# Four conditioned transformer blocks on one core: attention output of jobs 4 to 14 kept feature-major, divided by sums spread from HBM

## The reference

```python
# block 1 (16 heads of 16; l2-normalised q and k), block 2 (layernorm, 16 heads), block 3 (16 heads, no FFN)
scores = einsum('bhqd,bhkd->bhqk', q, k)
probs  = softmax(scores)                       # block 3: / sqrt(256)
o      = einsum('bhqk,bhkd->bhqd', probs, v)   # then back to [batch, tokens, 256]
x      = x + gate * (o @ proj_w + proj_b)      # blocks 1 and 2; block 3: x + ...
x      = x + gate * (gelu(norm(x) @ w1 + b1) @ w2 + b2)   # blocks 0 to 2
```

## Time and profile before

| | us |
|---|---|
| three executions | 1038.36, 1040.29, 1041.56 (median 1040.29) |
| the profiled execution, its own time | 1039.13 |
| its span, first to last instruction | 1037.5 |
| TensorE matmul busy | 1015.6 (98%) |
| ScalarE busy | 797.7 (77%) |
| VectorE busy | 705.3 (68%) |
| GpSimd busy | 492.5 (47%) |
| mean granted clock of TensorE | 0.997 of 2.4 GHz |

### The profile page before, as it was taken

One profiled execution on the slowest core, in us unless ns is written; L12 is line 12 of the kernel. 1 busy time (PEld: TensorE's weight loads), 2 busy tenths in 40 slices (PEclk: granted clock), 3 DMA queues, 4 the chain that ended last, 5 costly groups with the idle time before them and its releaser, 6 DMA issues.

```text
span 1037.5 us, 19799 instructions
## 1 busy us (share of the span) xinstructions
PE 1015.6 (98%) x6761; PEld 670.7 (65%) x6761; DVE 705.3 (68%) x1436; ACT 797.7 (77%) x1335; POOL 492.5 (47%) x446
## 2 busy tenths in 40 slices
PE   7999999999999999999999999999999999999995
PEld 5789898756657656676566566576666566545442
DVE  7765469563571563547857866967857857999984
ACT  3585756698898899887787887888877877787783
POOL 2563864716556256526346455345353355444241
PEclk9999999999999999999999999999999999999998
DMA  7010001405305132223033222222202203332220
GB/s 261 3 50 12 1 21 45 117 5 133 88 11 144 32 71 66 53 59 72 14 80 99 58 76 63 75 60 54 69 3 63 60 4 98 70 85 57 68 58 26
DMA packets 36386, 64.46 MB, mean 62 GB/s; under 512 B 7208, under 2 KB 22312, under 8 KB 36288
## 3 DMA queue, kind: packets, MB, share of 16 engines
q1 hardware_dynamic: 36288, 63.20, 23.5%
HBM read 22.90 MB, written 2.12 MB: 24 GB/s over the span
## 4 chain that ended last, share of the span: by engine, by line
PE 91%; POOL 2%; issue 2%; DVE 2%; DMA 1%; SPq 0%; ACT 0%; DVEq 0%; POOLq 0%
PE rings L565 17%; PE AVB L677 17%; PE rings L567 15%; PE rings L566 15%; PE rings L664 11%; PE rings L639 7%; PE rings L608 2%; PE rings L717 2%; PE rings L589 1%; PE rings L729 1%; PE rings L647 1%; DMA gT_f<-in_wqkv 1%; PE rings L692 1%; PE rings L627 1%; PE rings L601 1%
## 5 line engine op out<-in xcount | busy, mean ns | idle before, releaser
L876 ACT ACTIVATE probs<-rings 128x512 f32<-128x512 f32 x574 | 303.3, 610 | 85.0 <-PE rings L664 57.8
L1199 DVE TENSOR_REDUCE m<-rings 128x1 fp32r<-128x512 f32 x378 | 239.3, 682 | 52.8 <-PE rings L639 48.0
L677 PE MATMUL AVB<-probs,V 128*32 128x512 f32 x1536 | 200.9, 602 | 0.9 <-issue 0.9
L664 PE MATMUL rings<-SQ,SK 64*128 64x512 f32 x768 | 179.1, 438 | 1.9 <-DMA SQ<-cT 1.6
L1320 POOL TENSOR_TENSOR gT_l<-gT_f,gT_h 128x512 fp32r<-128x512 f32 x96 | 122.0, 1299 | 105.4 <-ACT gT_h L936 104.7
L664 PEld LDWEIGHTS rings<-SQ,SK 64*128 64x128 f32 x768 | 83.5, 184 | 94.5 <-issue 40.5
L639 PE MATMUL rings<-SK,SQ 63*128 63x512 f32 x512 | 129.5, 432 | 0.6 <-DVE m L1196 0.5
L565 PE MATMUL rings<-w_h,gT_h 128*128 128x256 f32 x384 | 111.4, 290 | 0.4 <-POOL gT_l L1320 0.4
L566 PE MATMUL rings<-w_l,gT_h 128*128 128x256 f32 x384 | 106.8, 278 | 0.0
L567 PE MATMUL rings<-w_h,gT_l 128*128 128x256 f32 x384 | 106.8, 278 | 0.0
L873 ACT ACTIVATE probs<-rings 128x1024 f32<-128x1024 f32 x97 | 95.5, 1044 | 4.9 <-issue 3.0
(11 more groups left out here) (198 smaller groups left out, 2177.2 us busy)
## 6 DMA issues: line engine op xcount, KB each, us to landing
SQ<-qh SPq DMA_DIRECT2D x96, 128.0 KB, 2.6
SK<-kh SPq DMA_DIRECT2D x96, 128.0 KB, 2.7
SQ<-ql SPq DMA_DIRECT2D x48, 128.0 KB, 2.7
SK<-kl SPq DMA_DIRECT2D x48, 128.0 KB, 3.0
raw<-in_w SPq DMA_DIRECT2D x20, 256.0 KB, 2.8
wmod_s<-in_wmod SPq DMA_DIRECT2D x6, 512.0 KB, 4.7
gates<-gate_rows SPq DMA_DIRECT2D x12, 256.0 KB, 3.6
raw<-in_wqkv SPq DMA_DIRECT2D x9, 256.0 KB, 2.8
```

Of the source, the lines that this page charges most:

```text
L664: mm = pe.matmul(o[:, :], SK[a % 4][r:r + KS + 1, n // 2, c * P:(c + 1) * P], SQ[a % 4][r:r + KS + 1, n // 2, :], start=True, stop=True)
L677: mm = pe.matmul(AVB[32 * n:32 * n + 32, :], V[j % 2][:, i, (HD + 1) * h:(HD + 1) * h + 32], probs[:, (4 * t + n) % PROBS, :], start=(i == ...
L876: act.activation(probs[:, n % PROBS, :], bank(kind, a, i)[:, :], ACT.Exp, scale=SCALE[layer(unit_job(a))]).then_inc(done["scores"], 1)
L1199: nc.vector.tensor_reduce(m16[:, col:col + 1], bank(kind, a, i)[:, :], AX_X, ALU.max, negate=True).then_inc(done["max"], 1)
```

## The change

For jobs 4 to 14 (`moved`) the steps oT1 and oT2 are replaced by seven kinds that leave the output feature-major; job 15 keeps oT1 and oT2.

- V is laid out anew, 18 x 16 columns: heads h and h + 8 lie interleaved, features at every second column, so that in the 32 rows of a head in AVB its features stand in the even rows and its sum in row 15. ScalarE writes V with a step of two elements.
- `take` (4 per job, one DMA of 128 KB each): the 64 even partitions of `oU[:, g, :]` go to half the partitions of `oc`, which is `tok2` seen as two tiles of features x 512 tokens. It waits for the unit's copy and for hT2 of the job before.
- `sums` (one DMA, 32 KB): the four sum rows of `oU` (4 x 2048) go to `rsum`, 64 partitions x 128. `turn`: VectorE's reciprocal on it. `back` (one DMA, 32 KB): to the HBM tensor `turned`.
- `spread` (2 per job, two DMAs of 128 KB each): from `turned`, each row of 512 repeated over the 16 features of its head, into `rc`, which is `tmp`. It waits for `back` and for fc2 of the job before.
- `divide` (2 per job): VectorE multiplies `oc` by `rc`, in place. `oN` (2 per job): ScalarE adds the bias and rounds into `postT_h`, VectorE makes `postT_l`, both from `oc`.
- proj waits for oN in place of oT2, norm2 too. TURNS is written anew as a whole, from the first step on.

The core of the diff (TURNS left out but for its last string):

```diff
+    moved = range(BATCH, JOBS - 1)
-              "gatecast": (many, 1), "oT1": (many, TT), "oT2": (many, CH), "hT2": (ffn, CH), "fc1": (ffn, MT),
+              "gatecast": (many, 1), "oT1": (jobs[-1:], TT), "oT2": (jobs[-1:], CH),
+              "take": (moved, UNITS), "sums": (moved, 1), "turn": (moved, 1), "back": (moved, 1), "spread": (moved, CH), "divide": (moved, CH), "oN": (moved, CH), "hT2": (ffn, CH), "fc1": (ffn, MT),
...
+    "s3 F j m2 a s x4 t m2 s2 jb t m3 U s3 m a s3 m2 a m2 s3 m2 a m2 s3 m2 js2 a s m3 s3 t s2 l X t m2 J l s4 m2 a2 "
+    "J s2 m2 s m2 p2 s6 a s B s m3 a M T3 s3 t s2 t a s3 a s7 W a2 s4 F W s4 W a2 T s2 W a2 A2 o4 O2 p2 B D2 T D W "
+    "D T2 W T W2",
...
+        oc = tok2[:, :, :].rearrange("p (c t) d -> p c (t d)", c=CH)
+        rc = tmp[:, :, :].rearrange("p (c t) d -> p c (t d)", c=CH)
...
+                elif kind == "take":
+                    sp.wait_ge(unit_out, UNITS * (a - BATCH) + i + 1)
+                    if layer(a - 1) < LAYERS - 1:
+                        sp.wait_ge(pe_ring, use("hT2", a - 1, CH - 1))
+                    else:
+                        sp.wait_ge(out_sem, 16 * nth("final", a - 1, TT - 1))
+                    r = 64 * (i % 2)
+                    sp.dma_start(oc[r:r + 64, i // 2, :], oU[0:P:2, i, :]).then_inc(taken[i], 16)
+                elif kind == "sums":
+                    sp.wait_ge(unit_out, UNITS * (a - BATCH + 1))
...
+                    src = bass.AP(s.tensor, s.offset, [[32 * UNITS * TOK, 4], [1, UNITS * TOK]])
+                    sp.dma_start(rsum[:, :], src).then_inc(summed, 16)
+                elif kind == "back":
+                    sp.wait_ge(done["turn"], nth("turn", a))
...
+                    sp.dma_start(turned[a % 2].rearrange("(p k) -> p k", p=64), rsum[:, :]).then_inc(back_out, 16)
+                elif kind == "spread":
+                    sp.wait_ge(back_out, MOVED_IN(a))
+                    if layer(a - 1) < LAYERS - 1:
+                        sp.wait_ge(done["fc2"], nth("fc2", a - 1, 1))
+                    else:
+                        sp.wait_ge(done["divide"], nth("divide", a - 1, CH - 1))
+                    s = turned[a % 2]
+                    for half in range(2):
+                        src = bass.AP(s.tensor, s.offset + TOK * (2 * i + half), [[UNITS * TOK, 4], [0, HD], [1, TOK]])
+                        sp.dma_start(rc[64 * half:64 * half + 64, i, :], src).then_inc(spread_in[i], 16)
...
+                            dst = bass.AP(v.tensor, v.offset, [[TT * VW, P], [HD + 1, 2], [2 * HD + 2, 8], [2, HD]])
...
-                    if g == 0 and j > BATCH:
-                        act.wait_ge(pe_ring, use("oT1", j - 1, TT - 1))
+                    if j > BATCH:
+                        act.wait_ge(taken[g], MOVED_IN(j - 1))
+                        act.wait_ge(summed, MOVED_IN(j - 1))
...
+                elif kind == "oN":
+                    act.wait_ge(done["divide"], nth("divide", a, i))
...
+                    act.activation(postT_h[:, i, :], oc[:, i, :], ACT.Identity,
+                                   bias=colv[:, layer(a), C_V + i:C_V + i + 1]).then_inc(hi_in[kind], 1)
...
+                elif kind == "turn":
+                    dve.wait_ge(summed, MOVED_IN(a))
+                    nc.vector.reciprocal(rsum[:, :], rsum[:, :]).then_inc(done[kind], 1)
+                elif kind == "divide":
+                    dve.wait_ge(spread_in[i], 2 * MOVED_IN(a))
+                    for g in (2 * i, 2 * i + 1):
+                        dve.wait_ge(taken[g], MOVED_IN(a))
+                    nc.vector.tensor_tensor(oc[:, i, :], oc[:, i, :], rc[:, i, :], ALU.mult).then_inc(done[kind], 1)
+                elif kind == "oN":
+                    nc.vector.scalar_tensor_tensor(out=postT_l[:, i, :], in0=oc[:, i, :],
...
-                        dve.wait_ge(pe_ring, use("oT2", a, CH - 1))
+                        dve.wait_ge(done["oN"], nth("oN", a, CH - 1))
```

More of the change, by code:

```diff
@@ L218 @@
 for _s in PLAN:
-    if _s[0] in ("hT2", "oT2") and _s[2] == 0:
+    if _s[0] in ("hT2", "oT2", "oN") and _s[2] == 0:
         POST_READ[_s] = _reader
@@ L349, in bank @@
             return ring[USE[(kind, a, i)] % RING]
-        kinds = sorted({s[0] for s in PLAN if not s[0].startswith("load") and s[0] not in ("stack", "crow", "store", "gelu", "gateout", "gatecast", "gatefix", "fold")})
+        kinds = sorted({s[0] for s in PLAN if not s[0].startswith("load") and s[0] not in ("stack", "crow", "store", "gelu", "gateout", "gatecast", "gatefix", "fold", "take", "sums", "back", "spread")})
         done = {k: sem("done_" + k) for k in kinds}
@@ L359, in cond_blocks_kernel @@
         sq_ready = sem("sq_ready")
-        hi_in = {k: sem("hi_" + k) for k in ("hT1", "hT2", "pT0", "oT2")}
+        hi_in = {k: sem("hi_" + k) for k in ("hT1", "hT2", "pT0", "oT2", "oN")}
         w_hi = sem("w_hi")
@@ L388, in cond_blocks_kernel @@
         final_dve = sem("final_dve")
+        taken = [sem(f"taken{g}") for g in range(UNITS)]
+        summed, back_out = sem("summed"), sem("back_out")
+        spread_in = [sem(f"spread_in{c}") for c in range(CH)]
         hi_v0 = sem("hi_v0")
@@ L560, in claim, with post_ready @@
                 return ring[n % RING]
+            def post_ready(a, n):
+                kind = "oN" if a < JOBS - 1 else "oT2"
+                return done[kind], nth(kind, a, n)
             def product(out, stationary, moving, first, last):
@@ L718, in _ @@
                 elif kind == "oT2":
[L719 to L729 removed]
+                    for t in range(2):
+                        pe.wait_ge(done["oT1"], nth("oT1", a, 2 * i + t))
+                        for c in range(CH):
+                            mm = pe.transpose(o[:, DIM * c + t * P:DIM * c + (t + 1) * P],
+                                              tok2[:, 2 * i + t, c * P:(c + 1) * P], ident[:, :])
                 elif kind == "proj":
[L731 removed]
+                    pe.wait_ge(*post_ready(a, 0 if a < JOBS - 1 else i))
                     pe.wait_ge(done["split_wp"], nth("split_wp", layer(a)))
@@ L1028, in _ @@
                         dve.wait_ge(pe_av, nth("av", UNITS * (a - 1) - 1, TT - 1))
-                        sums = V[a % 2][:, :, 0:VW].rearrange("p t (h e) -> p t h e", e=HD + 1)[:, :, :, HD:HD + 1]
-                        nc.vector.memset(sums, DIM ** 0.5).then_inc(done[kind], 1)
+                        for first in (2 * HD, HD - 1):
+                            ins = nc.vector.memset(V[a % 2][:, :, first:first + 7 * (2 * HD + 2) + 1:2 * HD + 2], DIM ** 0.5)
+                        ins.then_inc(done[kind], 1)
                 elif kind == "gate":
@@ L1064, in _ @@
                     dve.wait_ge(hi_in[kind], nth(kind, a, i))
-                    if a == JOBS - 1:
-                        tok = slice(DIM * i, DIM * (i + 1))
-                        for c in range(CH):
-                            ins = nc.vector.scalar_tensor_tensor(out=postT_l[:, c, tok], in0=bank(kind, a, i)[:, DIM * c:DIM * (c + 1)],
-                                                                 scalar=colv[:, layer(a), C_V + c:C_V + c + 1],
-                                                                 in1=postT_h[:, c, tok].bitcast(F32),
-                                                                 op0=ALU.add, op1=ALU.subtract)
-                    else:
-                        ins = nc.vector.scalar_tensor_tensor(out=postT_l[:, i, :], in0=bank(kind, a, i)[:, :],
-                                                             scalar=colv[:, layer(a), C_V + i:C_V + i + 1],
-                                                             in1=postT_h[:, i, :].bitcast(F32), op0=ALU.add, op1=ALU.subtract)
@@ L1076, in _ @@
-                    ins.then_inc(done[kind], 1)
+                    tok = slice(DIM * i, DIM * (i + 1))
+                    for c in range(CH):
+                        ins = nc.vector.scalar_tensor_tensor(out=postT_l[:, c, tok], in0=bank(kind, a, i)[:, DIM * c:DIM * (c + 1)],
+                                                             scalar=colv[:, layer(a), C_V + c:C_V + c + 1],
+                                                             in1=postT_h[:, c, tok].bitcast(F32),
+                                                             op0=ALU.add, op1=ALU.subtract)
```

63 lines of the change are left out of this document (31 added, 32 removed), and 78 rows, old and new, of tables (CODE, TURNS).

## The result

| | before | after |
|---|---|---|
| median of the executions side by side, us | 1040.5 (1038.4 to 1041.6) | 1060.0 (1058.6 to 1062.8) |
| ratio, 95% interval | | 1.019, 1.017 to 1.021 |
| span of the profiled execution, us | 1037.5 | 1061.0 |
| TensorE matmuls | 6761 | 6497 |
| TensorE busy, us | 1015.6 | 1018.6 |

What follows compares the result with a forecast made beforehand. It took TensorE to bound the kernel up to job 12's last AV and VectorE behind it. 1039.1 - 23.0 + 2.3 + 3.2 + 3 = 1024.6, plus 1.2 for the median: 1026 us, range 1013 to 1039.

Steps and rivals of the forecast that it cites:

- The new chain: Sums to spreads after a job's last AV, jobs 4 to 14: mostly hidden, +3 us for all jobs.
- every leg at 3.6 us: Upper end for the transfers from sums to spreads: first landing at 12.6 us, 1.5 us a job, 16 in all.
- the 2 that I had named as the limit: VectorE before a divide: forecast wrong if divides wait over 2 us a job.
- -23.0 us: Order before job 12's last AV: 27.4 us of TensorE steps removed or left for later, 4.4 given back.
- +2.3 us: Behind job 12's last AV: VectorE's work rises from 158.5 to 160.8 us and sets the time.
- So up to there TensorE's own work is the time: Up to job 12's last AV (869.39 us), TensorE's pitches sum to only 13 us short of the trace.
- rival 2: ScalarE takes over in layer 1, VectorE from layer 2's end: 1033 us as priced, 1037 at worst; chance 0.17 for both.
- There VectorE sets the time: From job 12's last AV to TensorE's last matmul, 158.8 us: VectorE's work makes 158.5, TensorE's pitches 150.4.
- +3.2 us: Divides and subtractions reading two SBUF inputs beside GpSimd: 0.26 us each, 12 of them where VectorE binds.
- the 855 that I had named: Sign: forecast wrong if job 12's last AV comes later than 855 us.
- Rival 4: Before the divides: few DMA engines carry the spreads, they land late and VectorE stands; 50 us, 1076 us; chance 0.10.
- Rival 3: SP's queue delays the shift rows: one late unit in four of 32, 10 us, 1036 us; chance 0.12.

Runs made afterwards that it cites:

- with distinct rows: The change with its spreads reading 64 distinct rows of x instead of 4 rows 16 times each, division left out: 1037.0 us, 0.997 of the kernel before.
- experiment 8, last run: The change with 256 KB spreads from sixteen rows (sums written back twice), sums fetched early except in job 10: 1036.7 us, 0.9965 of the kernel before.

## Why the prediction was wrong

Two steps of the sum failed, and one term did not appear.

**"The new chain", +3 us: 24 measured** (1060.0 against 1036.3 without the chain). The step that failed is "the first pair of spreads 3.6 (the broadcast of the gates from HBM, 256 KB, is the nearest)". That row has 128 distinct rows on the receiving side and one source row; the spread has four source rows outermost. By themselves the four spreads of a job take 8.3 us, in the kernel 9.2; the first pair has landed after 6.0 us, not 3.6, and the second after 9.2, not 4.8. The legs before them came as summed (7.8 against 7.6, where the terms named for it, 4, 0.69 and twice 1.3, add up to 7.3). My upper end, "every leg at 3.6 us" and 16 us in all, took each leg for independent of the others; but the spreads land one behind another, as if on the same four engines. The waits at the divides came out at 2.4 us a job, past the 2 that I had named as the limit. On top comes what the sum had no term for: TensorE behind each stand works at 1.2 GHz. In the change there are 30.7 us of it against 10.2 with distinct rows, so at most 10 of the 23 us between them; by the rate of the filled stands (2.6 to 4.1 us for 17) I estimate 3 to 5.

**"-23.0 us" and "+2.3 us" for the order: some 5 gained instead of 20.7** (1035.3 with takes, divides and chain left out). In that run job 12's last AV comes 8.3 us sooner than before, not 23.0, and what is behind it is 4.4 us longer, not 2.3. "So up to there TensorE's own work is the time, and what is taken off it is gained": that inference failed. TensorE's pitches made up the trace to 13 us of 869, and still three quarters of what was taken off came back as waits, in the old order as well (5.3 of 21.8; up to job 12's last AV 4.5 of 15.8). That a sum of pitches fits shows only that TensorE never stood long, not that the others would have been ready sooner. The reading that fits is that ScalarE, VectorE and TensorE run round seven banks at nearly one pace: halving work of both the others gave 18 us. It is not shown bank by bank, and 27 us over the pitches stay unexplained. My rival 2 said something near it, ScalarE in layer 1 (the halving shows it in job 7 alone) and VectorE from layer 2's end, priced at 1033, and without the late spreads its time would have been right to 2 or 3 us; with 0.17 I held it too unlikely. "There VectorE sets the time", of the stretch behind job 12's last AV, was too sharp as well: taking 15 us of divides off VectorE, 4.2 of them in the last stage, gained nothing, and in the change it was busy 91% of the last stage, not over 95.

**"+3.2 us" for operations with two SBUF inputs: nothing.** The divides have a median of 692 ns and one of 22 lasted 1782; the subtractions have a mean of 748, as in the earlier trace rows. Without the divides the time stayed. The trace says why: the wait that I had seen is there, but hardly ever met. Of these 44 instructions two start inside a GpSimd operation, one with 0.2 us of it left (752 ns), and the other is the long one:

```profile
904.88 1.78 DVE L1135 TENSOR_TENSOR tok<-tok,tmp 128x512 f32<-128x512 f32 x1
...
903.61 2.51 POOL L1444 TENSOR_TENSOR X<-X,rowp 128x512 f32<-128x512 f32 x2 [10.38 <-DMA rowp<-in_rows]
```

In the fastest version above (experiment 8, last run) a divide that starts with 0.66 us of a GpSimd operation left takes 1.21 us and a subtraction with 0.95 left 1.50. So it is paid by what is left of the other operation, and my "0.26 us each" was the rate of four products that lay in a dense run of GpSimd work.

**Right:** the reciprocal on 64x128 takes 0.95 us; the divide 0.69 for 0.68; the write back 2.0 for 1.8; and SP's queue stayed under the limit set for it: scores waited 8.1 us in all for a shift's row, against 10, in five places and mostly at units 37 and 53. Job 12's last AV, at 881.8 us, is far behind the 855 that I had named, but so it is without any chain (860.6): that sign pointed at the order, not at the spreads.

**Rival 4 was the mechanism**, given 0.10. Its price of 1.9 us a spread is near what was measured (steps of 2.2, 1.8 and 1.4 us in the kernel, 1.6 by themselves), its last landing, 17.8 us behind the AV, came at 17, the engines are four, and it came to 2.2 us a job, not 4.5: VectorE stood 2.4 us a job before both divides together and 1.1 before the reciprocal, less than the 6 that I had worked out before the second divide alone. "Against it: the nearest broadcast, of 128 rows, takes 3.6 us" was no evidence, since that row differs in just the thing on which the rival hangs. Nor was it true that nothing of the old trace shows how many engines carried a DMA: the same increments can be counted there. Each broadcast of the gates makes 16, each load into four partitions (`rowg<-in_rows`) five, and the listing gives no landing time for just those with fewer than 16. Rival 3, at SP's queue, is in the result as well (units 37 and 53).

The rule of the Trainium skill (DMA: Bandwidth & Descriptors, Why a DMA increments its semaphore by 16 and not by 1), that the number of engines is the largest up to 16 which divides the outermost counts, agrees with every row here: 4, 8 and 16 engines' landings for spreads of 4, 8 and 16 rows, and by themselves 8.3 us for four rows, 5.3 for eight, 4.5 for 64. The 27 GiB/s per engine of the same page (Specifications), by which I estimated 1.1 us for each spread, don't: the measured step is 1.6 us for 32 KB an engine by itself. I had the rule in hand and let a row that didn't bear on it outweigh it.

## What to carry to other kernels

Look at the outermost count of a DMA's source before costing it by its bytes: spreads from four rows took 8.3 us for what spreads from eight do in 5.3, and a second copy of 32 KB in HBM, which makes sixteen rows, with the sums fetched earlier, turned 1060 us into 1037. Removing work from the busiest engine need not be worth its own time, and the way to know is to leave the work out of the *old* kernel and time it: here a quarter. A landing time that is missing from a listing is worth a look: here it marked just the DMAs that few engines carried. And in a queue that stands in order, every wait on SP has to be read with what is queued behind it; one fetch that was moved forward cost 9 us.

## What the runs showed of the hardware that I had not expected

TensorE's clock fell to 1.2 GHz behind single stands of 3.2 to 3.7 us, and stayed at 2.4 GHz when the stands were filled with products whose results nobody reads; the filling made the kernel 2.6 to 4.1 us faster. Behind a run of short stands it fell too (0.42 us each at 422 to 424 us in the change). A fetch of 32 KB from four partitions takes 2.3 us by itself, nearly as long as 128 KB from 64 rows of HBM (2.5): by the landings, it too is carried by four engines. And a VectorE instruction with two inputs in SBUF that starts inside a GpSimd operation is longer by what is left of that operation less some 0.15 us (a divide 1782 ns with 1.24 us left and 1211 with 0.66 left, against 692), where that operation works on tiles of 256 or 512 columns.
